# Turning to pixels inside the sets of the forward part, and a factor applied as the blocks leave PSUM

## The reference

```python
skip = xin + _layer_norm(om, ln1_g, ln1_b)
ffn = jax.nn.gelu(skip @ ffn_w1 + ffn_b1, approximate=False) @ ffn_w2 + ffn_b2
out = skip + _layer_norm(ffn, ln2_g, ln2_b)
```

## Time and profile before

| What | us |
|---|---|
| median of 3 runs | 852.76 |
| lowest and highest | 852.08, 854.6 |
| profiled execution, its own time | 854.39 |
| its span | 852.6 |
| forward part, first PE instruction to the last DVE one | 499.3 to 700.9 |
| turning part | 701.1 to 742.6 |
| tail | 742.6 to 852.6 |

### The profile page before, as it was taken

The page is one execution under the profiler, slowest core; times in us unless marked ns, Lnnn a source line. Parts: engine busy times, 40 slices in busy tenths (PEclk is TensorE's granted clock), DMA queues, the critical chain, the costliest instruction groups (busy, mean ns, idle before and its releaser), DMA issues. The chain is left out here.

```text
span 852.6 us, 21573 instructions
## 1 busy us (share of the span) xinstructions
PE 727.2 (85%) x8482; PEld 387.7 (45%) x8482; DVE 520.7 (61%) x964; ACT 488.0 (57%) x986; POOL 374.6 (44%) x464
## 2 busy tenths in 40 slices
PE   3676589999999999999998569999999657749587
PEld 2454155555555555555555222333333227734254
DVE  3566156666767767776668212677777966671145
ACT  3433346777777777777775448877777206723000
POOL 4467355767776677767776520021111233300000
PEclk9999879999999999999999959999999758969989
DMA  7351000000000000000000020021111203000378
GB/s 180 81 143 35 10 2 2 2 3 3 2 3 2 2 3 2 2 3 2 3 2 2 2 50 1 25 50 52 50 50 50 68 12 90 0 1 1 55 144 281
DMA packets 15436, 31.38 MB, mean 37 GB/s; under 512 B 7208, under 2 KB 9004, under 8 KB 15340
## 3 DMA queue, kind: packets, MB, share of 16 engines
q1 hardware_dynamic: 14216, 29.61, 13.9%
q10 hardware_dynamic: 856, 0.20, 0.2%
q0 software_dynamic: 272, 0.27, 0.2%
HBM read 20.70 MB, written 9.37 MB: 35 GB/s over the span
## 5 line engine op out<-in xcount | busy, mean ns | idle before, releaser
L757 POOL TENSOR_TENSOR sc<-sc,mx 128x512 f32<-128x512 f32 x128 | 133.8, 1045 | 34.2 <-DVE mx L705 34.2
L702 DVE TENSOR_TENSOR sc<-s_ps,bias_tab 128x512 f32<-128x512 f32 x128 | 87.6, 684 | 59.2 <-PE s_ps L532 59.2
L655 ACT ACTIVATE pt<-t_ps 128x512 f32<-128x512 f32 x128 | 76.0, 594 | 52.6 <-PE t_ps L543 51.4
L1199 POOL TENSOR_TENSOR square<-xs 128x1024 f32<-128x1024 f32 x16 | 33.8, 2111 | 162.1 <-DVE xs L1101 162.1
L705 DVE TENSOR_REDUCE mx<-sc 128x8 f32<-128x512 f32 x128 | 87.8, 686 | 4.4
L1018 ACT ACTIVATE hs<-h_ps,fb1s 128x512 f32<-128x512 f32 x128 | 78.2, 689 | 17.7 <-PE h_ps L932 17.6
L543 PEld LDWEIGHTS t_ps<-consts,sc 128*128 128x128 f32 x512 | 53.7, 141 | 73.1 <-issue 45.9
L543 PE MATMUL t_ps<-consts,sc 128*128 128x128 f32 x512 | 83.9, 286 | 2.2 <-ACT pt L655 1.6
L532 PE MATMUL s_ps<-kx,qu 32*64 32x128 f32 x2048 | 71.4, 276 | 1.5 <-DVE sc L702 1.4
L932 PE MATMUL h_ps<-xs,fw 64*128 64x512 f32 x256 | 68.5, 649 | 1.0 <-ACT hs L1018 1.0
L945 PE MATMUL c_ps<-hs,fw 128*64 128x512 f32 x256 | 62.0, 604 | 0.8 <-DVE fcsq L1045 0.7
(11 more groups left out here) (190 smaller groups left out, 1402.1 us busy)
## 6 DMA issues: line engine op xcount, KB each, us to landing
raw<-in_x_dram SPq DMA_DIRECT2D x32, 256.0 KB, 4.2
xr<-in_x_dram SPq DMA_DIRECT2D x32, 256.0 KB, 3.9
out_dram<-x SPq DMA_DIRECT2D x32, 256.0 KB, 3.7
rec_scratch<-r SPq DMA_DIRECT2D x4, 224.0 KB, 4.8
xs<-rec_scratch SPq DMA_DIRECT2D x4, 224.0 KB
w<-in_L_conv_W_dram SPq DMA_DIRECT2D x1, 784.0 KB
w<-in_L_conv_W_dram SPq DMA_DIRECT2D x1, 672.0 KB
consts<-in_c_consts_dram SPq DMA_DIRECT2D x1, 400.0 KB, 3.8
```

The source lines that it names most:

```text
L655: act.activation(pt[a][2 * hp + j][:, :, :], t_ps[:, :, :], ACT.Exp).then_inc(s["exped"], 1)
L702: dve.tensor_tensor(sc[n % KEPT][:, :, :, :], s_ps[j][:, :, :, :], bias_tab[:, j, hp], ALU.add)\
L757: pool.tensor_tensor(v, v, mx[n % KEPT][:, :].unsqueeze(2).broadcast_to([128, 8, TOK]), ALU.subtract)\
```

## The change

The turning part goes away, and its work becomes part of the steps of the forward part, a set after the set's sum of squares is there:

- `centre` writes the pair in block order already, in four instructions of 256 columns instead of one of 1024. `fold_square` sums 256 columns instead of 128.
- The pair is turned without its factor. For each set, `turn_var` (2 tiny matmuls) makes the variances with image columns on the partitions, ACT's `turn_rstds` does Ln and Exp on 4 numbers a partition, `spread_pixels` (2 tiny matmuls) spreads the factors to the 128 pixels of a block, and DVE's `copy_pixel_rstd` brings them to SBUF.
- `turn_fill` turns 3, 3 and 2 blocks of a pair, so 6 fills a set with 16 matmuls, into one bank `t_ps`. DVE's `turn_out` multiplies by the factor as it takes the blocks out of PSUM (one instruction for `yt`, one for `raw_scores`). A fill waits for the `turn_out` before it; in the last set two banks alternate.
- The bank for this was one of the two `r_ps`. `spread_rstd` is now one matmul at a time, four times a set, each waiting for the `scale` before it, which the steps place apart.
- There are two more steps (n up to 12). The tail's weights are loaded from the tail's own block on, POOL's zeroing too, and the waits for those loads move from the start of DVE's work there to where the weights are used. The table of indices (`iota`) is loaded in the forward part.

```diff
-                    for k in range(2):
-                        r = rows(2 * half + k)
-                        last = pe.matmul(r_ps[k][:, :], spread_image[r], rv[r, :], start=True, stop=True)
-                    last.then_inc(s["rstd_ps"], 1)
+                    after(pe, s["scaled"], 4 * b + k)
+                    pe.matmul(r_ps[:, :], spread_image[rows(k)], rv[rows(k), :], start=True, stop=True)\
+                      .then_inc(s["rstd_ps"], 1)
...
+            TURN_FILLS = ((0, 2, 4), (1, 3, 5), (6, 7))
...
+            def turn_fill(pe, b, i):
...
+                    elif b == SETS - 1:
+                        pe.wait_ge(s["turn_out"], 6 * b + i - 1)
+                    else:
+                        pe.wait_ge(s["turn_out"], 6 * b + i)
+                    for m, gp in enumerate(TURN_FILLS[i % 3]):
+                        last = pe.matmul(turn_bank(b, i)[:, TURN * m:TURN * (m + 1)], xs[:, p, 128 * gp:128 * (gp + 1)],
+                                         turn[:, gp], start=True, stop=True)
+                    last.then_inc(s["turned"], 1)
...
-                dve.tensor_tensor(xs[:, p].rearrange("c (h w) -> c h w", w=W),
...
+                    for y in range(4):
+                        last = dve.tensor_tensor(xs[:, p].rearrange("c (y x h w) -> c y x h w", y=4, x=4, h=WS)[:, y],
...
+            def turn_out(dve, b, i):
...
+                    dve.tensor_tensor(yt[:, p, take].rearrange("c g (a n) -> c g a n", a=2),
+                                      src[:, :, 0:128].rearrange("c g (a n) -> c g a n", a=2),
+                                      factor.unsqueeze(3).broadcast_to([128, cols, 2, C]), ALU.mult)
+                    dve.tensor_tensor(raw_scores[:, p, take].rearrange("c g (b a) -> c g b a", a=2),
...
-            STEPS = range(SETS + 3)
+            STEPS = range(SETS + 5)
...
             def tensor_step(pe, n):
                 hidden(pe, n, 0, 0)
                 hidden(pe, n, 0, 1)
+                turn_fill(pe, n - 5, 3)
                 pair_mean(pe, n - 3, 1)
+                spread_rstd(pe, n - 2, 2)
                 output(pe, n - 1, 3)
+                turn_fill(pe, n - 5, 4)
                 hidden(pe, n, 1, 0)
```

More of the change, by code:

```diff
@@ L899, in build @@
                 "w_in", "zero", "chain", "b2_mean", "hid_ps", "gelu", "out_ps", "out", "csq", "var_ps", "ln", "rstd",
-                "rstd_ps", "scaled", "update", "placed", "sum_ps", "sums", "mean", "centred", "square", "sq_ps", "sqsum")}
+                "rstd_ps", "scaled", "update", "placed", "sum_ps", "sums", "mean", "centred", "square", "sq_ps", "sqsum",
+                "turn_var", "turn_rstd", "pixel_ps", "pixel_rstd", "turned", "turn_out")}
             FORWARD_LINKS = 6
             SETS = UNITS // 4
+            turn = sb(stage, "turn", [128, 8, TURN])
+            cw_in = sb(stage, "cw_in", [128, BLOCKS])
+            sqsums = sb(stage, "sqsums", [128, PAIRS, W])
+            to_pixels = sb(stage, "to_pixels", [W, 2, 128])
             x_back = [sem(stage, f"x_back{k}") for k in range(2)]
@@ L1007, in pair_square_sum @@
                         pe.wait_ge(s["sqsum"], 2 * b + 1)
-                    sum_rows(pe, square[:, k]).then_inc(s["sq_ps"], 1)
+                    for e in range(2):
+                        for g in range(4):
+                            at = 128 * (2 * g + e)
+                            last = pe.matmul(n_ps[rows(g), 128 * e:128 * (e + 1)], group_rows, square[:, k, at:at + 128],
+                                             start=True, stop=True)
+                    last.then_inc(s["sq_ps"], 1)
@@ new lines, in build, with turn_var @@
+            TURN_FILLS = ((0, 2, 4), (1, 3, 5), (6, 7))
+            def turn_var(pe, b):
+                if there(b, SETS):
+                    pe.wait_ge(s["sqsum"], 2 * b + 2)
+                    after(pe, s["turn_out"], 6 * b)
+                    for k in range(2):
+                        last = pe.matmul(t_ps[0:W, 2 * k:2 * k + 2], sqsums[:, 2 * b + k], spread_image[:, 0:128:C],
+                                         start=True, stop=True)
+                    last.then_inc(s["turn_var"], 1)
@@ new lines, in spread_pixels, with turn_bank @@
+            def spread_pixels(pe, b):
+                if there(b, SETS):
+                    pe.wait_ge(s["turn_rstd"], 2 * b + 2)
+                    for e in range(2):
+                        last = pe.matmul(t_ps[:, 4 * e:4 * e + 4], to_pixels[:, e],
+                                         turn_rstd[:, :, :].rearrange("w k a -> w (k a)"), start=True, stop=True)
+                    last.then_inc(s["pixel_ps"], 1)
+            def turn_bank(b, i):
+                return r_ps if b == SETS - 1 and i % 2 else t_ps
@@ L1037, in rstds, with turn_rstds @@
                     act.activation(rv[:, :], rv[:, :], ACT.Exp, scale=-0.5).then_inc(s["rstd"], 1)
+            def turn_rstds(act, b):
+                if there(b, SETS):
+                    act.wait_ge(s["turn_var"], b + 1)
+                    after(act, s["pixel_ps"], b)
+                    small = turn_rstd[:, :, :].rearrange("w k a -> w (k a)")
+                    act.activation(small, t_ps[0:W, 0:4], ACT.Ln, bias=eps[0:W, 0:1]).then_inc(s["turn_rstd"], 1)
+                    act.wait_ge(s["turn_rstd"], 2 * b + 1)
+                    act.activation(small, small, ACT.Exp, scale=-0.5).then_inc(s["turn_rstd"], 1)
             def square_output(dve, i, k):
@@ L1122, in tensor_step @@
                 hidden(pe, n, 1, 1)
-                spread_rstd(pe, n - 2, 1)
+                turn_fill(pe, n - 5, 5)
+                spread_rstd(pe, n - 2, 3)
+                turn_var(pe, n - 4)
                 variances(pe, n - 1)
@@ L1127, in tensor_step @@
                 hidden(pe, n, 2, 1)
+                spread_pixels(pe, n - 4)
                 pair_sum(pe, n - 2, 0)
@@ L1426, in _ @@
                     sp.wait_ge(s["stored"], 32 * PAIRS)
+                @block.gpsimd
+                def _(pool):
+                    pool.memset(ow[:, :], 0.0).then_inc(tail_zero, 1)
+                    pool.memset(st_t[:, :, :], 0.0)
+                    for t in range(2):
+                        last = pool.memset(r[:, t], 0.0)
+                    last.then_inc(tail_zero, 1)
                 @block.vector
```

179 lines of the change are left out of this document (81 added, 98 removed).

## The result

| | before | after |
|---|---|---|
| median us (4 runs each, same chip) | 853.68 | 892.66 |
| lowest and highest | 852.08, 856.47 | 890.29, 895.6 |
| span of the profiled execution | 852.6 | 892.0 |

The ratio is 1.0444, with a 95% interval from 1.0405 to 1.0484: 39 us slower. The forecast was 890 with a range of 866 to 906.

A forecast was written before the change was run, and what follows sets the result against it. PE was taken as packed in the forward part's sets. Turning part -41.5, forward part up to the last `variances` +40.3, drain +38.8 make +37.6 us; on the median 852.76 this gives 890, range 866 to 906.

The forecast's parts named there:

- Single spreads: Up to the last `variances`, 14 pairs of spreads become 28 single ones at 1.02 us: 13.7 us added, bounds 9.2 and 14.8.
- Rival 3: New matmuls overlap their neighbours on PE, a single spread costing 0.53: 841 us, faster; chance 0.03 in full.
- Early fills: Fills of 8 of 16 pairs before the last `variances`, 64 matmuls in 24 groups: 17.5 us, bounds 15.5 and 19.
- Tiny matmuls: `turn_var` and `spread_pixels` before the last `variances`, 9 twos at 0.45 us: 4.1 us, bounds 2 and 6.1.
- Waits: New PE waits up to the last `variances`, at a set's first spread and the fifth fill: 5 us, bounds 0 and 10.
- Drain: After the last `variances`, four pieces at the lower clock, taken as 71 us instead of 32.2: 38.8 added, bounds 12.8 and 48.
- Rival 1: Fills keep PE busy enough that the drain runs at the full clock: 55 us instead of 71, total 874; chance 0.2.
- DVE: Full steps: DVE needs 20.3 us a set of about 29, staying under PE and costing only through its order.
- rival 4: Full steps: DVE becomes the bound if `turn_out` takes twice 0.63 us: +10, 900; chance 0.17 shared with another rival.
- rival 2: Some 60 PE groups before the last `variances` cost a further 0.2 us each: +12, 902; chance 0.17 shared with another rival.
- Tail: In the tail the weights' loads are hidden and POOL's zeroing costs 0 to 0.7 us: counted as 0.
- `place` starting later into POOL's square: In the drain, `update` and `turn_out` before `place` lessen its 2.15 us beside POOL's square (0.89 alone); counted inside 27 and 21.

The follow-up runs named there:

- e1: Kernel before with one bank for the spread factor, four single spreads a set instead of two pairs, `scale` and `update` moved; 877.02 us, ratio 1.0268.
- e8: Kernel after with filler matmuls that nothing reads on PE in the drain, none from step 12 on; 883.99 us, ratio 1.033.
- e2: Kernel after without the fills and takings out of PSUM of sets 0 to 3, factors still made; 875.61 us, ratio 1.0272.
- e3: Kernel after without the fills and takings out of PSUM of sets 4 to 7, factors still made; 861.59 us, ratio 1.0095.
- e4: Kernel after with filler matmuls that nothing reads ahead of PE's waits in the drain, some behind the last fill; 892.32 us, ratio 1.0425.
- e7: Kernel before with filler matmuls ahead of PE's waits in the drain and of the turning part's first fill; 852.27 us, ratio 0.9977.
- e9: Kernel before, spread pairs kept, all 16 pairs turned in the drain through four banks, ACT's later factor batches made early; 834.73 us, ratio 0.9766.

## Why the prediction was right

The forecast was 890 and 892.66 was measured, and its mechanism is what the runs show: a packed PE that pays each new slot, a few waits for DVE, and a drain with one bank at the lower clock. By the prediction's own steps:

- *Single spreads*: put at 1.02, bounds 0.86 and 1.06; measured 1.05 in after and in e1. For 28 less 14 pairs that is 14.6 instead of 13.7. Rival 3 (0.53, overlap) falls. Its sum had a slip besides: the 16.5 that it leaves before the last variances is reached only with the fills at their lower bound of 15.5, and with 17.5 it is 18.5.
- *Early fills*: put at 17.5; 16 x 0.87 + 8 x 0.65 = 19.1 at most. Two of the six fills of a set stand beside the mean, which has their form (128*128), and there the two are cheaper together: fill and mean take 1.10 (600.78 to 601.88) and 1.01 (611.30 to 612.31) instead of 0.87 + 0.34 = 1.21. For four sets that is 1.2 less, 17.9.
- *Tiny matmuls*: put at 4.1; five `turn_var` at 0.1 and four `spread_pixels` at 0.53 are 2.6. A `turn_var` nearly disappears: its row starts at 591.46, that of the `variances` behind it at 591.55.
- *Waits*: put at 5. The slots leave 40.1 - 14.6 - 17.9 - 2.6 = 5.0, and PE's waits in the rows say the same: 6.49 us after (0.36 to 0.50 at the first spread of a set, 0.45 at the fifth fill, 0.95 twice in step 8, 0.35 once for `sqsums`) against 1.45 before, each without the 1.02 at the first `hidden`. Up to the last `variances` 40.1 against 40.3; the four terms missed by +0.9, +0.4, -1.5 and 0.0, so a part of the fit is that the tiny matmuls, put too high, made up for spreads and fills.
- *Drain*: pieces 27, 21, 14 and 10 were 27.2, 21.8, 14.6 and 9.4. The whole was taken at 71, though the pieces add up to 72, and measured 72.9. Rival 1, the full clock, didn't happen. Had it, e8 shows 62.4 with the fillers, where I had 55 without: 22, 17, 10 and 6.5 against 23.1, 18.7, 12.9 and 7.6. The fillers are in the latter, so the clock alone is worth 10 us or more; whether my 17 is right no run shows.
- *DVE*: a `turn_out` of three blocks was 0.55 + 0.16 long, its slot 0.54 (718.42 to 718.96 below), put at 0.63; `centre` 1.42, put at 1.5. In a full step DVE is busy for 18.86 of 29.56 us, so rival 4 falls. In the drain the round of fill and `turn_out` at the lower clock was put at 2.2 and measured 2.41 in set 6 (1.69 for the fill, where I had 1.44, and 0.73 until the next). Two of the six fills of set 6 ran at the upper level, so the six took 12.2 us where I had 12: a round too short and a clock too low made up for each other there.
- *Change of shape* (rival 2, 12 us more): the slots and waits of the packed steps add up to what was measured, with nothing left for a further 0.2 a change. The row 605.42 (a fill between a sum and an `output`) has a slot of 0.87 for 3 x 0.242 = 0.73 of stream, 0.14 for its start. The row 611.30, with the mean of the same form behind it, has a slot of 0.78. The trace agrees with the direction of the rule in the Trainium skill (TensorEngine Tiling (Array Packing), Key Properties): a change of form costs some 0.1 us here.
- *Tail*: put at 0, measured +1.3. The copy of the scores takes 0.92 us beside POOL's zeroing and 0.59 without; the rest is less than the tail differs by between the profiles (108.6 to 112.5). The weights' loads are hidden.

The prediction also counted on `place` starting later into POOL's square. DVE's rows show how much that helped; POOL's squares run from 717.92 to 720.25 and from 728.68 to 731.01:

```profile
718.42 0.56 DVE L1205 TENSOR_TENSOR xs<-f_t_ps,pixel_rstd 128x384 f32<-128x384 f32 x1
718.88 0.17 DVE L1208 TENSOR_TENSOR raw_scores<-f_t_ps,pixel_rstd 128x12 f32<-128x12 f32 x1
718.96 2.05 DVE L1149 TENSOR_TENSOR x<-xr,fcc 128x336 f32<-128x336 f32 x4
...
729.85 0.55 DVE L1205 TENSOR_TENSOR xs<-f_t_ps,pixel_rstd 128x384 f32<-128x384 f32 x1
...
730.39 1.37 DVE L1149 TENSOR_TENSOR x<-xr,fcc 128x336 f32<-128x336 f32 x4
```

`place` still takes 2.05 where it starts 1.0 us into the square, hardly less than the 2.15 of the earlier trace rows, and 1.37 where it starts 1.7 us into it; both times it ends 0.75 us behind the square, not far from the 0.89 that it takes alone. `turn_out`, with one input in PSUM, takes 0.56 and 0.55 inside the two squares and 0.56 at 763.43, where POOL does nothing. The trace agrees with what the prediction took from the Trainium skill (SBUF — State Buffer, Who interferes with whom) on both.

The parts measured by leaving them out, by windows, make the same sum. In the forward part: single spreads 17.0 (e1), early half 19.7 (e2), tiny matmuls 2.6, together 39.3, and 40.1 was measured. In the drain: single spreads 1.8 (e1) and late half 31.5 (e3); the 7.4 that remain of the 40.7 are a difference and were not measured by themselves.

## What to carry to other kernels

Work that leaves a part of its own for a part where one engine is packed costs its full slot there, and the bank that it takes away can cost as much as the work: here about 19 us, beside about 20 for the half of the turning that stands in the packed steps. Look instead for the stretch where that engine has room and where many PSUM banks are free, since with one bank matmul and take-out alternate and each pays for the other. How much a low clock matters depends on what the stretch waits for: some 2 us of 32 in the old drain, where DVE was busy for 25, and at least 10 of 73 where fills and take-outs alternated. And fillers that hold up the clock must not stand where real work is about to come, or behind the last of it: at the end of the drain they hid a gain in e4 and in e7.

## What the runs showed that I had not expected

- Four banks in the drain gave 22 us, where I had expected 8. They end the alternation and with it most pauses of PE, and the clock came up by itself, from 0.58 to 0.77. PE's busy time over the drain fell from 56.6 to 41.9 us for the same matmuls.
- At the full clock the old drain was only 2 us shorter up to its last `centre` (e7), though PE's own matmuls there take up to twice as long at the lower level (a pair of spreads 2.08 against 1.13), and the fillers at its end took that again.
- An ACT activation of 128 columns with a scale column takes 0.37 us, one of 4 columns still 0.26. ACT's four instructions for a fill of two blocks come to 0.96 us from one fill to the next (e9, 712.42 to 713.38), DVE's two to 0.5. In e9 ACT is busy for 39.3 and DVE for 35.8 of the 51.5 us, so 10 pairs to 6 is near an even share: DVE has the rest of the forward part to do as well.
